# Last graph layer: picked rows in a PSUM bank, one bank for the way out, another order on PE

## What is computed

```python
def _L3_gnn_ref(x, edge_index):
    msgs = x[edge_index[1]]
    out = jax.ops.segment_sum(msgs, edge_index[0], num_segments=x.shape[0])
    return out
...
h = jnp.maximum(_layernorm(x, axis=-1), 0.0)
x = x + _L3_gnn_ref(h, edge_index)
```

## Time and profile before

| | us |
|---|---|
| median of three runs | 2092.9 |
| the three runs | 2078.06, 2093.66, 2092.9 |
| the profiled execution | 2089.63 |
| its span | 2087.9 |
| last layer, from the first gather to the last evacuation | 1722 to 2045 |

### The profile page before, as it was taken

How to read it: one execution, slowest core, us unless ns; L and a number is a source line. 1 busy time by engine, 2 the same in 40 slices (tenths; PEclk the granted TensorE clock), 3 DMA queues, 4 the chain that set the end, 5 groups by cost and what they waited for, 6 DMA issues and landing times. The chain is left out here.

```text
span 2087.9 us, 24015 instructions
## 1 busy us (share of the span) xinstructions
PE 1574.6 (75%) x7395; PEld 1202.0 (58%) x7395; DVE 1519.1 (73%) x2399; ACT 901.3 (43%) x1184; POOL 1390.2 (67%) x1404
## 2 busy tenths in 40 slices
PE   2777877777566787888787169999987529999990
PEld 1555555555454665666565157777764317878880
DVE  6777767777674677777786677777768658999992
ACT  1333333333226676776753125555537413444430
POOL 5777777777637777777774557777750317777764
PEclk9966766667567999999998579999995559999995
DMA  5422223223223555554553424444455313434332
GB/s 125 109 77 82 82 72 87 73 81 86 67 56 103 159 167 157 157 175 157 168 168 128 107 61 93 99 94 94 93 109 189 107 24 75 102 93 113 94 94 52
DMA packets 216475, 220.63 MB, mean 106 GB/s; under 512 B 107230, under 2 KB 170163, under 8 KB 216115
## 3 DMA queue, kind: packets, MB, share of 16 engines
q1 hardware_dynamic: 167603, 147.32, 23.6%
q0 software_dynamic: 45024, 58.36, 13.4%
q10 hardware_dynamic: 3744, 13.63, 1.7%
HBM read 117.72 MB, written 101.46 MB: 105 GB/s over the span
## 5 line engine op out<-in xcount | busy, mean ns | idle before, releaser
L609 POOL DMA_INDIRECT gathered<-table,idx x1272 | 1271.6, 1000 | 511.3 <-issue 397.2
L1704 DVE COPY_PREDICATED spare<-spare,psum 64x512 f32<-64x512 uint8 x294 | 216.6, 737 | 117.5 <-ACT spare L1318 108.0
L964 PE MATMUL psum<-rounded 128*128 128x512 f32 x1144 | 272.7, 395 | 22.1 <-DVEq L1697 22.1
L964 PEld LDWEIGHTS psum<-rounded 128*128 128x128 f32 x1144 | 212.9, 189 | 65.6 <-DVEq L1697 22.5
L642 POOL DMA_INDIRECT arena<-scan,rowidx x100 | 104.8, 1048 | 152.5 <-DMA scan<-ea 94.5
L1734 DVE TENSOR_TENSOR_SCAN arena<-arena,psum 128x512 f32<-128x512 f32 x52 | 66.3, 1275 | 151.1 <-PE psum L881 150.6
L1318 ACT ACTIVATE spare<-psum 64x512 f32<-64x512 f32 x82 | 48.3, 590 | 295.6 <-PE psum L964 295.1
L1113 ACT ACTIVATE arena<-psum 128x1024 f32<-128x1024 f32 x52 | 53.2, 1024 | 242.5 <-PE psum L732 149.4
L881 PE MATMUL psum<-ident,arena 128*128 128x128 f32 x352 | 63.9, 338 | 99.0 <-ACT arena L1219 99.0
L1716 DVE TENSOR_SCALAR_CACHE_REDUCE rounded<-spare,rowcol 128x1024 fp32r<-128x1024 uint16 x110 | 134.4, 1269 | 0.2
L881 PEld LDWEIGHTS psum<-ident,arena 128*128 128x128 f32 x352 | 55.5, 238 | 133.6 <-ACT arena L1219 129.7
(11 more groups left out here) (273 smaller groups left out, 3512.0 us busy)
## 6 DMA issues: line engine op xcount, KB each, us to landing
scan<-arena SPq DMA_DIRECT2D x52, 768.0 KB, 4.7
scan<-ostage SPq DMA_DIRECT2D x130, 256.0 KB, 2.2
gathered<-table,idx POOLq DMA_INDIRECT x1272
d_mlp<-arena ACTq DMA_DIRECT2D x26, 512.0 KB, 2.7
arena<-d_mlp SPq DMA_DIRECT2D x52, 256.0 KB, 3.1
ea<-in_edge_attr SPq DMA_DIRECT2D x104, 128.0 KB
spare<-src_row SPq DMA_DIRECT2D x98, 128.0 KB, 3.6
spare<-src_quarter SPq DMA_DIRECT2D x98, 96.0 KB, 3.0
```

Source lines behind the costliest of these rows:

```text
L609: pool.indirect_dma_start(out=out[:, j, hf, :], out_offset=None, in_=tab[layer], in_offset=bass.IndirectOffsetOnAxis(ap=idx[:, j, hf * NCH ...
L964: last = nc.tensor.matmul(P[:, bank + t, :], parts[layer][n][:, b:b + 2, :].rearrange("p b d -> p (b d)"), tile(layer, m, u)[:, hf * CH:(h ...
L1704: picked = v.copy_predicated(rows[m % 2][halves[hf], :], quarter[m % 2][halves[hf], q - 1, :], P[halves[q % 2], bank + q // 2, :])
```

## The change

All of it is in the last layer. The picked rows of a multiplied chunk are put together in PSUM bank 4, of which there is one, and no longer in two SBUF tiles: ACT's first quarter and DVE's picks write there and the scan reads from there. The first quarter of m therefore waits for the scan of m-1. The ins use banks 5 and 7 and all outs bank 6, so an out waits for the evacuation of the chunk before it. On PE the out of the multiplied chunk goes between the first half of the next multiply and the ins; on ACT its evacuation goes behind the first quarter of half 0 and ahead of the one-hots. DVE's order stays.

```diff
+        def picked_rows(layer, m):
+
+            return P[:, 4, :] if layer == 3 else rows[m % 2]
...
             def l3_out(i, k):
                 pe.wait_ge(S("scanned", k), n_scanned(3, i + 1))
-                pe.wait_ge(S("evacuated", k), n_evacuated(3, i))
+                pe.wait_ge(S("evacuated", 1 - k), n_evacuated(3, i + k))
                 for j in range(J):
-                    last = nc.tensor.transpose(P[:, 6 + k, j * 128:(j + 1) * 128], scanb[k][:, j::J], ident[:, :])
+                    last = nc.tensor.transpose(P[:, 6, j * 128:(j + 1) * 128], scanb[k][:, j::J], ident[:, :])
...
-                    last = nc.tensor.transpose(P[:, 4 + g % 2, j::J], pair(g % 2, g // 2 % 2, j), ident[:, :])
+                    last = nc.tensor.transpose(P[:, 5 + 2 * (g % 2), j::J], pair(g % 2, g // 2 % 2, j), ident[:, :])
...
                     multiply(3, m + 1, 0, 0)
+                l3_out(c // 2, c % 2)
                 for other in after(3, m):
                     l3_in(other)
                 if m + 1 < len(MULTIPLIED[3]):
                     multiply(3, m + 1, 1, 2)
-                for done in (c, *after(3, m)):
+                for done in after(3, m):
                     l3_out(done // 2, done % 2)
...
-                nc.scalar.activation(rows[m % 2][halves[hf], :], P[0:64, bank, :], ACT.Copy) \
+                nc.scalar.activation(picked_rows(layer, m)[halves[hf], :], P[0:64, bank, :], ACT.Copy) \
...
                 if m < len(MULTIPLIED[3]):
-                    if m >= 2:
-                        before = MULTIPLIED[3][m - 2]
-                        act.wait_ge(S("scanned", before % 2), n_scanned(3, before // 2 + 1))
+                    if m:
+                        act.wait_ge(S("scanned", c % 2), n_scanned(3, c // 2 + 1))
                     first_quarter(3, m, 0, 0)
+                if m:
+                    evacuate(3, c // 2, c % 2, 6)
+                if m < len(MULTIPLIED[3]):
                     if 0 < m < len(MULTIPLIED[3]) - 1:
                         distances_and_onehots(3, m + 1)
                     first_quarter(3, m, 1, 2)
                 if m:
-                    for done in (c, *after(3, m - 1)):
-                        evacuate(3, done // 2, done % 2, 6 + done % 2)
+                    for done in after(3, m - 1):
+                        evacuate(3, done // 2, done % 2, 6)
...
-                    picked = v.copy_predicated(rows[m % 2][halves[hf], :], quarter[m % 2][halves[hf], q - 1, :],
+                    picked = v.copy_predicated(picked_rows(layer, m)[halves[hf], :], quarter[m % 2][halves[hf], q - 1, :],
                                                P[halves[q % 2], bank + q // 2, :])
...
-                    made = rows[m % 2]
+                    made = picked_rows(3, m)
...
-                    made = P[:, 4 + g % 2, :]
+                    made = P[:, 5 + 2 * (g % 2), :]
```

## The result

The changed kernel takes 2090.3 us, the kernel before 2083.4 us (medians of 20 runs each, on the same chips). The ratio is 1.0032 with a 95% interval of 1.0016 to 1.0048: slower by a third of a per cent, 6.7 us, and between 3 and 10 us. The forecast was +7.8 us and 2098. The direction and the new loop were right. The level was set between the profiled execution and a median of three runs, 6.2 and 9.5 us over the median of 20. In the last layer, where all of the change is, 4.8 to 6.0 us were lost and not 7.8: the picks into PSUM, which the forecast put at nothing, gave 3.8 us back, and the end cost 0.7 us more than forecast.

A forecast was written before the change was run, and what follows sets the result against it. PE and DVE were taken to bound the last layer together, POOL close behind. Groups +8.3, start −1.8 and end +1.3 gave +7.8 us: 2097.4 on the profiled execution, 2100.7 on the median, said as 2098, range 2083 to 2116.

The forecast's parts named there:

- the new loop: Last layer: DVE's scan, ACT's first-quarter copy and DVE's next pick form a loop, leaving DVE idle about 0.73 us.
- The level: Whole time said as 2098 us, from 2097.4 on the profiled 2089.6 and 2100.7 on the median 2092.9.
- the end: Last chunk: scan 51 begins 1.36 us behind scan 50, as its in-transpose follows chunk 50's out; +1.3 us.
- What bounds: Last layer: PE (69.4 us busy) and DVE (67.5) together bound the 71.4 us period, POOL's gathers close behind.
- the list of signs: Expected last-layer waits: first quarter 25 to 32 us, PE's third out about 0.5 us, 8 times; period 73.3 us.
- The groups and the start: Last layer: 13 groups of two +0.47 us, 8 of three +0.27, sum 8.3; less 1.8, mostly for PE-led first groups.
- Where the data lie: Moving picks, ACT copies and scan sources to PSUM in the last layer was taken to change nothing, 0 us.
- The lower bound of that step: Picks into PSUM in the last layer might take 0.05 us less each, giving back 3 to 5 us.
- the prediction's own sign of being wrong: Wrong if picks left 0.74 us, the last layer's period stayed at 71.4 us or fell, or POOL began to wait.
- The sum: Last layer's total: 8.3 for the groups, less 1.8 at the start, plus 1.3 at the end, +7.8 us.
- the faster one: PE's gain decides: 8 groups of three save 4.9 us, 1.3 lost at the end, about 2086 us; chance 0.12.
- Dear picks: Picks into PSUM cost more, about 11 us per 0.1 us a pick, up to about 2155 us; chance 0.13.

The follow-up runs named there:

- one swap of two lines: The changed kernel with the ins of a group put ahead of its first out again: ratio 1.0007 to the kernel before, scans 302.2 us.
- the outs in place: Against the changed kernel, every out goes back to the bank its scan read, ins first, two row banks: ratio 0.9955 to the kernel before, scans 296.7 us.
- the same order and the rows in SBUF: Against the changed kernel: ins ahead of the early first out, two out banks, rows in two SBUF tiles with the old wait; ratio 0.9995 to the kernel before.

## Why the prediction was right or wrong

Point by point, against the scans' length, which is free of the clock at the start:

- *What bounds.* Right: PE and DVE bound the stage together, and taking 0.7 us from PE in a group of three (2.69 to 1.96) brought nothing while DVE was given more.
- *The new loop.* Right, with its size: 0.70 us for 0.73, and 1.24 for 1.23 behind a group of three; all waits for the first quarter are 24.5 us, where 25 to 32 were forecast. PE's wait at the third out is 0.78 us, 8 times, as the sum had it (T+0.60 to T+1.35); the 0.5 us in the list of signs does not follow from that sum.
- *The groups and the start.* The forecast for all but the end was 8.3 − 1.8 = 6.5 us with picks unchanged. The kernel with picks in SBUF has 8.6, of which 2.0 are the end: 6.6. Its period was 73.13 for 73.35. That the two agree to 0.1 us is in part luck: by the ends of the multiplied scans the first four groups grew by 1.1 us and not by 0.4, and the others by 5.5 and not by some 6.1.
- *The end.* Mis-sized: 1.3 us forecast, 2.0 measured (2.08 against 0.08). I had used the out and in rows of the running stage, at a granted clock of 1.00; they ran at 0.50, and took 1.13 and 0.87 us for 0.75 and 0.44. With the new order alone the same two ran at 1.00 after as long a pause, and scan 51 came 1.28 us behind scan 50, near the forecast's 1.36. The kernel before held the sign: its own last outs took 1.04 and 1.13 us at granted clocks of 0.63 and 0.50.
- *Where the data lie.* This is the step that failed: "So I take nothing." The pick into PSUM took 699 ns and not 740, and moving the rows to PSUM, with ACT's copies (568 ns for 590), gave back 8.6 − 4.8 = 3.8 us. So the period grew by 0.75 us and not by 1.95. The lower bound of that step, 3 to 5 us given back at 0.05 us a pick, was the true one, and the prediction's own sign of being wrong, picks of another duration, came true. The one write to PSUM in the earlier trace rows has its source in SBUF and is another operation; two short rows were no ground for zero.
- The sum: 6.5 + 2.0 − 3.8 = 4.7, measured 4.8 in the scans and 6.0 in the stage; the 1.2 us between them are the first multiplies, which were slower in the one profile. The 1.2 us follow the granted clock of 0.74 and 0.50. The ratio says 6.7 (3 to 10) us, which holds both lengths and the forecast's 7.8; that 7.8 lies so near 6.7 is luck, since the layer does not have it. Whether the change does anything outside the last layer is not shown, and nothing in it is changed there.
- *The level.* 2098 was wrong: it lay between the profiled execution plus the sum and the median of three plus the sum, and these stood 6.2 and 9.5 us above the median of 20 runs. From that median to 2098 it is 14.6 us, more than twice what was measured. Set on 2083.4, the sum gives 2091.2, and 2090.3 was measured. Nor is 1% the least that can be told apart, as the prediction held: 20 runs of each kernel told 0.3%.
- *The rivals.* Of the faster one only its premise was there: PE's gain in a group of three exists (0.7 us for the 0.6 forecast), and the layer is longer all the same. Dear picks were ruled out by their rows. That POOL would not wait held: it waited 0.3 us once.

## What to carry to other kernels

When two engines share the bound, merging two buffers into one on the side that is not quite the bound makes it the bound: count the round trip (here 0.04 + 0.57 + 0.10 us) into every turn. An in-order engine should do the work that waits for nothing before the work that waits: one swap of two lines was worth 5.9 us of 308 in the scans, where giving up an out bank, taking the new wait and moving the rows to PSUM together cost 2.6 (299.6 to 302.2). A result can go back into the bank that its source has just left, which here removed the wait for the scan before and the wait for the out bank, with no bank more. And the price of an operation whose output moves to another memory has to be measured or given a range that the forecast uses. Short PE work behind a pause is priced from rows at the clock that is granted there.

## What was not expected of the hardware

*The picks.* A 64x512 predicated copy took 0.04 us less with its output in PSUM (699 against 734 to 740 ns), and ACT's copy from PSUM 568 ns into PSUM against 590 into SBUF. For ACT that is the direction of what the Trainium skill says ("ScalarE: Activation LUTs", "Step-by-step: what each stage is for"), that ScalarE is nearer to PSUM; here that is worth 4%. The same place puts VectorE nearer to SBUF, by which a pick into PSUM should be the dearer one; here it is 5% cheaper, and the measurement decides.

*POOL and the scans.* The 240 gathers of the layer took 7 us less in all four kernels with the rows in PSUM. As one group of instructions, before has 234.6 us and 978 ns; the changed kernel has

```profile
L613 POOL DMA_INDIRECT gathered<-table,idx x240 | 227.6, 948 | 115.9 <-issue 72.5 <-DMA table<-arena 43.1 <-PE psum L1068 0.3
```

and the six others with the rows in SBUF have 970 to 990 ns. In the profile before, 13 gathers are longer than 1.1 us. One is the first of the layer (2.09 us; after, the first takes 2.06 us and no other is long). The other 12 are all those that start 0.1 to 0.9 us behind the start of a scan with both keep and rows in SBUF, and each of them ends 0.75 us behind that scan's end, whenever it began. They take 1.15 to 1.92 us where 0.945 is usual, 6.9 us more in all, which is the whole difference of the two rows. Timeline before:

```profile
1886.86 1.28 DVE L1912 TENSOR_TENSOR_SCAN scan_ring<-keep,scan_ring,spare 128x512 f32<-128x512 uint8 x1
...
1887.49 1.41 POOL L609 DMA_INDIRECT gathered<-table,idx  x1 [0.30 <-issue]
```

A scan whose rows come from PSUM reads one tensor from SBUF, and no gather beside it was long. The Trainium skill ("SBUF — State Buffer", "Who interferes with whom") has this rule: a DVE instruction with two SBUF inputs contends with a GpSimd instruction that reads SBUF. The traces agree, with 0.2 to 1.0 us a meeting. The reverse shows too: 7 scans of that form beside which a gather began within their first 0.07 us took 1311 to 1330 ns, the other 15 at most 1285, and those from PSUM at most 1282. POOL was not the bound here, so this gave the changed kernel nothing; with the outs in place, whose period is 69.8 us, it is close to it. By the row above a gather takes 0.95 us and its issue gap 72.5 / 240 = 0.30, and the 56 gathers of a period 56 x 1.25 = 70 us. In that kernel they took 70.06 us. With the same order and the rows in SBUF, prolonged gathers and all, 56 gathers took 70.9 to 72.7 us in a stage whose period was 70.5, so POOL's lead shrank, and PE's weight loads waited for a gather once, 0.4 us.
